# Passes over half of the queries, three banks for the maxima, and one exponential per head's bank

## What is computed

```
x = layer_norm(x, ln1)                      # the context, 6404 rows
lat = layer_norm(latents, ln2) * (1 + scale) + shift      # 1024 rows
q = lat @ Wq.T                              # 16 heads of 64
k, v = split(concat(x, lat) @ Wkv.T)        # 7428 keys
w = softmax((q / 64**0.25) @ (k / 64**0.25).T)
out = concat_heads(w @ v) @ Wo.T
```

## Time and profile before

| | us |
|---|---|
| median of 3 runs | 3836.62 (3833.6 to 3837.98) |
| the profiled execution | 3841.93 |
| its span, first to last instruction | 3840.2 |

### The profile page before, as it was taken

How to read it: one execution, slowest core, us unless ns; L and a number is a source line. 1 busy time by engine, 2 the same in 40 slices (tenths; PEclk the granted TensorE clock), 3 DMA queues, 4 the chain that set the end, 5 groups by cost and what they waited for, 6 DMA issues and landing times. The chain is left out here.

```text
span 3840.2 us, 51865 instructions
## 1 busy us (share of the span) xinstructions
PE 3356.3 (87%) x18323; PEld 1880.7 (49%) x18323; DVE 2607.8 (68%) x4176; ACT 1515.3 (39%) x1843; POOL 1641.2 (43%) x1061
## 2 busy tenths in 40 slices
PE   3896969668435699999999999999999999999977
PEld 2553636433232255555555555555555555554535
DVE  6887868765317877777777777778778778773221
ACT  4232313234220044444444444444444444444432
POOL 1222222201130055655555555556555555566650
PEclk9897969866666599999999999999999999999988
DMA  1000000000130000000000000000000000000000
GB/s 57 0 0 0 0 0 0 0 12 1 35 108 6 0 1 1 3 1 2 1 3 2 1 3 2 1 3 2 1 3 2 1 3 1 2 1 1 1 24 6
DMA packets 20389, 27.87 MB, mean 7 GB/s; under 512 B 5064, under 2 KB 12368, under 8 KB 20048
## 3 DMA queue, kind: packets, MB, share of 16 engines
q1 hardware_dynamic: 18832, 21.83, 1.8%
q0 software_dynamic: 1344, 3.15, 0.3%
HBM read 21.30 MB, written 3.67 MB: 7 GB/s over the span
## 5 line engine op out<-in xcount | busy, mean ns | idle before, releaser
L2140 POOL TENSOR_TENSOR pair_total_pool<-pair_total_pool,pair_probs 128x1024 f32<-128x1024 f32 (+2 forms) x456 | 1335.1, 2928 | 918.2 <-DVE pair_total L2104 880.0
L2027 ACT ACTIVATE pair_probs<-banks 128x1024 f32<-128x1024 f32 (+1 forms) x944 | 962.9, 1027 | 1137.0 <-PE banks L1921 1129.6
L2057 DVE TENSOR_REDUCE pair_peaks<-banks 128x1 f32<-128x512 f32 (+1 forms) x1680 | 1094.7, 673 | 238.6 <-PE banks L1902 198.2
L1945 PE MATMUL banks<-pair_probs,pair_values 128*64 128x512 f32 (+1 forms) x3776 | 863.1, 598 | 0.0
L1902 PE MATMUL banks<-pair_k_high,pair_q_high 64*128 64x512 f32 (+1 forms) x1920 | 706.4, 464 | 68.3 <-DVE pair_peaks L2050 51.1
L2104 DVE TENSOR_TENSOR pair_total<-pair_total,pair_probs 128x512 f32<-128x512 f32 x464 | 445.5, 960 | 208.2 <-POOL pair_total_pool L2140 155.6
L1902 PEld LDWEIGHTS banks<-pair_k_high,pair_q_high 64*128 64x128 f32 x1920 | 306.9, 195 | 443.4 <-issue 354.8
L1921 PE MATMUL banks<-pair_q_shift,pair_one_rows 64*128 64x512 f32 (+1 forms) x1888 | 512.8, 432 | 6.1 <-ACT pair_probs L2027 5.9
L1921 PE MATMUL banks<-pair_q_high,pair_k_high 64*128 64x512 f32 (+1 forms) x1888 | 494.1, 392 | 0.0
L1921 PE MATMUL banks<-pair_q_high,pair_k_low 64*128 64x512 f32 (+1 forms) x1888 | 493.2, 391 | 0.0
L1945 PEld LDWEIGHTS banks<-pair_probs,pair_values 128*64 128x64 f32 (+1 forms) x3776 | 249.4, 136 | 463.6 <-issue 400.6
(11 more groups left out here) (312 smaller groups left out, 3281.5 us busy)
## 6 DMA issues: line engine op xcount, KB each, us to landing
expert_w<-in_fc SPq DMA_DIRECT2D x32, 256.0 KB, 3.9
context_rows<-in_ctx SPq DMA_DIRECT2D x10, 320.0 KB, 6.2
dense_w<-in_We SPq DMA_DIRECT2D x2, 1024.0 KB
experts_in<-expert_zeros SPq DMA_DIRECT2D x1, 1024.0 KB, 3.9
expert_b<-in_fc_b SPq DMA_DIRECT2D x2, 512.0 KB
expert_rows<-experts_in SPq DMA_DIRECT2D x16, 64.0 KB, 2.0
experts_out<-expert_result POOLq DMA_DIRECT2D x4, 256.0 KB, 4.5
row_parameters<-in_rows SPq DMA_DIRECT2D x1, 896.0 KB, 7.9
```

Source lines behind the costliest of these rows:

```text
L1945: last = pe.matmul(out[heads[head], c, :], values[0:n, (g * BLOCKS + i // 4) % 2, i % 4, heads[head]], probs_of(i)[0:n, c, head, :], start ...
L2027: act.activation(probs_of(i)[0:n, c], slot(e)[0:n], ACT.Exp, scale=1.0 / 8.0).then_inc(S["expd"].sem, 1)
L2057: v.reduce_max(peaks[:, head, t, b:b + 1], fill_banks(f)[:, head, 0:width(b)], axis=AX).then_inc(S["peaked"].sem, 1)
L2140: pool.tensor_tensor(pooled[0:rows_, first:3], pooled[0:rows_, first:3], probs_of(i)[0:rows_].rearrange("p c h n -> p (c h) n")[:, first + ...
```

## The change

The loop over pairs becomes a loop over 16 **halves**: a half is one pair of heads by 512 of the 1024 queries (h = 2g and 2g + 1). Each half runs through all keys, with its own queries, maxima, shift, denominators and output, all 512 wide where they were 1024.

- **Steps.** 15 per half. A step is one block of keys: four tiles (three in the last, the third being the remnant) by 512 queries, so again four scores entries, each with one fill of the next half. 60 fills against 59 scores: one stands alone ahead of the scores of the last step. Before the first half 60 fills run alone instead of 120.
- **Banks.** `out` is 512 wide and needs one bank; banks 5, 6 and 7 hold the fills in turn, so a fill of one head waits for the maximum three before it, where it waited for the maximum of its own head in the fill before.
- **Exponentials.** One for each head's bank (512 columns), head 1 first (FIRST). The first waits for `half_made`, set by the last product of head 1, the second for `made`. The next user of the slot that is a scores entry waits at each head's first product for that head's exponential, not ahead of the entry; other users wait for both.
- **Places.** (0, 0), (1, 0), (1, 0), (2, 0) for tiles 0 to 3 of a block: head 1's fill first, head 0's at position 0, 1, 1 or 2 of its products.
- **Keys and values** of a pair serve both halves, so they are kept (a ring of 16 blocks each; values had two). Keys and values of pair g+1 are made in the odd half of pair g, values two blocks behind keys. Those of pair 0 are made in the stage in front, with the keys and under one signal.
- **Sums.** VectorE takes tile 0 of a block and one bank of tile 1 (at the end the remnant), POOL the rest in two operations; at a half's end POOL also adds VectorE's total and its own third part, in three operations in a row, and the denominators are two matmul sums instead of five.
- **Reciprocals** in four pieces (CHUNKS = 4), output in step 6 instead of step 10.

The core of the diff:

```diff
-STEPS1 = TILES // 2
-RING1 = BLOCKS + 3
-CHUNKS = 8
-FIFTH = (16, 18, 20, 22)
-PLACES = ((0, 0), (0, 3), (0, 3), (1, 4))
+HALVES = 2 * PAIRS
+TQ = TT // 2
+HALF = TQ * P
+LAST = BLOCKS - 1
+RING1 = BLOCKS + 1
+CHUNKS = 4
+PLACES = ((0, 0), (1, 0), (1, 0), (2, 0))
+FIRST = (1, 0)
...
-        order += [("fill", 0, b, t) for t in range(TT)]
+        order.append(("produce", 0, b + 1, 0, b) if b < LAST else ("produce", None, None, 0, b))
+        order += [("fill", 0, b, t) for t in range(TQ)]
...
+    for h in range(HALVES):
+        g, more = h // 2, h + 1 < HALVES
+        ahead = [("fill", h + 1, b, t) for b in range(BLOCKS) for t in range(TQ)] if more else []
+        for s in range(BLOCKS):
+            if s == LAST and more:
                 order.append(ahead.pop(0))
+            for i in tiles_of(s):
+                order.append(("scores", h, i, ahead.pop(0) if ahead else None))
+            made = [None] * 4
+            if h % 2 and g + 1 < PAIRS:
+                if s < LAST:
+                    made[0:2] = [g + 1, s + 1]
+                if s:
+                    made[2:4] = [g + 1, s - 1]
+            elif h % 2 == 0 and s == 0 and g:
+                made[2:4] = [g, LAST]
+            elif h % 2 == 0 and s == LAST and g + 1 < PAIRS:
+                made[0:2] = [g + 1, 0]
...
+            elif s == LAST:
+                adds = [("add", h, i) for i in tiles_of(s - 1)]
+                if more:
+                    order.append(("peak", h + 1))
+                if h + 2 < HALVES:
+                    order.append(("queries", h + 2))
+                order += adds[0:1] + produce + adds[1:2]
+                if more:
+                    order.append(("shift", h + 1))
+                order += adds[2:4]
...
-        values = k.sb("pair_values", [P, 2, 4, P], ctx=ctx)
+        values = k.sb("pair_values", [P, RING1, 4, P], ctx=ctx)
...
-        out = k.ps[:, 4:6, :]
+        out = k.ps[:, 4, :]
...
-        def fills_before(f):
-            return fill_number[f] - (1 if f[1] else 2)
+        def fill_bank(f, head):
+            return k.ps[:, 5 + (2 * fill_number[f] + FIRST.index(head)) % 3, :]
...
                 def fill(f, head):
...
+                    n = 2 * fill_number[f] + FIRST.index(head)
+                    if h:
+                        wait(pe, "peaked", max(n - 2, 2 * first_fills))
...
                     def product(head, m):
...
+                        if m == 0:
+                            wait_free(e, FIRST.index(head))
                         return pe.matmul(slot(e)[0:n, head, :], left, right, start=m == 0, stop=m == 3)
...
+                        elif turn == (FIRST[0], 3):
+                            product(*turn).then_inc(S["half_made"].sem, 1)
+                        elif turn == (FIRST[1], 3):
                             product(*turn).then_inc(S["made"].sem, 1)
...
+                    for head in FIRST:
+                        if head == FIRST[1]:
+                            wait_made(act, e)
+                        act.activation(probs_of(h, i)[0:n, head], slot(e)[0:n, head], ACT.Exp,
+                                       scale=1.0 / 8.0).then_inc(S["expd"].sem, 1)
```

## The result

The changed kernel takes 3732.1 us, median of four runs (3730.5 to 3736.0), where the kernel before took 3837.3 beside it: a ratio of 0.9728 (95% interval 0.9711 to 0.9744). 3728 was forecast. The profiled execution has a span of 3728.7 us against 3840.2, so 111.5 us less; the sum of the prediction had 108.5. In medians it is 105.2 us less, since the profiled execution before lay above the other runs and the one after was the fastest of its four.

The account below looks back on a forecast made before the run. PE was busy 87% but stopped by VectorE and ACT in turns; VectorE bound the front stage. Terms -51 - 15 - 52 + 7.5 + 7 - 5 = -108.5 gave 3728 us; 8-in-10 range 3665 to 3795.

Parts of the forecast that it names:

- Part 1: Front stage: four fewer maxima a block, keys' copy waits for values; blocks 11.1 to 8.1 us, together -51 us.
- the case that the prediction priced at -59: Front stage with PE at its full clock, where the values would cost 1.0 us a block.
- Parts 2 and 5: Last pair: values made a pair ahead, -15 us; shorter end, -5; its score phases +7.5, borders about +1.
- Part 3: Four scores of a step: 5.10 us, bounds 4.75 to 5.28; three-score phases 4.5; -52 us over seven pairs.
- the layout: Score phase timed slot by slot: VectorE's stops gone, third score waits for head 0's second exponential until 2.61, adds at 5.10.
- Part 4: Borders, twice as many: changes of form and 0 to 1 us waits before denominators, +7 us, bounds -5 and +25.
- the -46 of the forecast: Pairs 0 to 6: -52 us from score phases and about +6 for borders.
- A: Score phases: waits merely change place, phase stays 5.27, +36 us, 3764 us; chance 0.20.
- B: Score phases: no wait is left, -74 us, 3654 us; chance 0.12.
- C: Waits before each head's first product: even fulfilled, they stop weights loading ahead, 0.8 a phase, +168, 3896 us; chance 0.08.
- D: Borders: PE sits through POOL's whole chain, 6 us at each of 16, 3817 us; chance 0.05.

Follow-up runs that it names:

- experiment 6: Changed kernel with head 0's exponential first and, in the front stage, values as an entry of their own behind a block's second fill: 3674.1 us, 0.9568.
- experiment 2: Changed kernel with one exponential over both banks: first kernel, behind two waits in a row, 3759.4 us, 0.9795; second kernel, behind one wait, 3747.8 us, 0.9766.
- experiment 7: Kernel of experiment 6 with one of the four adds put ahead of the production in each step that has one: 3693.4 us, 0.9618.
- experiment 3: Changed kernel with two banks for maxima: 3820.2 us; two banks and the fills' old places, mirrored: 3779.0 us; three banks and those old places: 3734.9 us.
- experiment 1: Changed kernel with ACT making head 0's exponential first and PE asking for the banks in that order: 3704.8 us, 0.9656.
- experiment 5: Changed kernel with each head's wait for its exponential asked again ahead of its third product, eight more fulfilled waits a phase: 3728.7 us, 0.9716.

## Why the prediction was right

**Part 1, the front stage: -54.5 for -51.** The mechanism was as written, VectorE held by the keys' copy and that by the values, and experiment 6 shows it by taking it away. The blocks were 7.1 to 8.3, 7.9 in the mean, instead of 8.1; PE's clock, 0.67 in the mean, was not always the half one, toward the case that the prediction priced at -59.

**Parts 2 and 5, the last pair: -12.3 for -11.5.** The values gave the 15 (productions of this pair on PE fell from 16.2 us to 1.0), and from the last products on the end is 4.7 us shorter, for 5. The phases cost 9.4 (133.0 before, 142.4 after) for 7.5, and the rest is -1.8 for +1. One row was carried over wrongly: phases without fills were to stay 4.38 and are 4.47, 14 x 0.09 = 1.3 us. In the third score the two heads' first products, which start together before, now follow one another:

```profile
3521.01 0.92 PE L1925 MATMUL banks<-pair_q_shift,pair_one_rows 64*128 64x512 f32 x2
```

Head 1 is in its slot, 1.94 behind the phase's start, and head 0, whose exponential is the second, is 0.42 behind head 1. But with a wide one behind one wait (second kernel of experiment 2) these phases are still 4.44, so the split accounts for 0.03 of the 0.09. The 0.06 that the wide one has over 4.38 are about what its exponentials start later than in the kernel before.

**Part 3, the phase: 5.11 for 5.10.** Each step of the layout is there: no stop of the second score, head 1's fill in its slot at +2.40, head 0's product at +2.60 (2.61 was laid out), the fourth score free. The three-score phase is 4.42 for 4.5. VectorE no longer releases a regular fill; it does in the three-score phase, for the 0.40 us that were allowed:

```profile
3478.30 0.38 PE L1906 MATMUL banks<-pair_k_high,pair_q_high 64*128 64x260 f32 x1 [0.40 <-DVE pair_peaks L2069]
```

The sum of a pair's score phases after is 151.9 for 151.8. The one of before was put at 159.2 from the earlier trace rows and is 160.1 when all phases are added: one phase of each pair but the first, the one behind the output, was 5.97 and was taken for a regular one. So the phases gave -8.2 a pair, not -7.4.

**Part 4, borders: inside its bounds, but too low, and wrong in where it lies.** I allowed +7 for waits ahead of the denominators and for changes of form at the borders. The waits view of PE over all pairs (engine line waited for: us in total, times, longest us), of before and of after:

```profile
PE banks L1902 <- DVE pair_peaks L2057: 14.6, 65, 0.7
PE banks L1921 <- ACT pair_probs L2027: 5.9, 29, 0.2
```
```profile
PE banks L1964 <- POOL pair_total_pool L2134: 9.8, 8, 4.9
PE banks L1906 <- DVE pair_peaks L2069: 6.9, 16, 0.9
```

Less the 4.9 of the last one, which is the end of the stage, PE waits seven times for POOL, 0.7 us each, inside the 0 to 1 allowed, at every second border; and VectorE stops fills 16 times instead of 65. The denominators' fewer columns nearly paid for the changes of form and the wait: shift, queries, denominators and output take 7.5 us a pair before, and 7.3 after with 0.7 of waiting beside them, so +0.5 a pair for the +0.9 that was allowed. But adds and productions, which I had left alone, grew by 0.8 and 0.4 us a pair. More of their groups now stand between matmuls of another form: at a half's end the adds and the production are put among each other. The sixteen matmuls of a step's adds take 3.58 us where nothing stands between them, and at a half's end 1.01 + 1.01 + 1.87 = 3.89. No run takes this away alone, but experiment 7 puts one more such change in each step and pays 0.15 for it. One term was missing. Pair 0 had no border in it before, since nothing was finished ahead of it; now its second half has one, some 4 us, and pair 0 gives 2.1 us where the others give 6.5. From the -46 of the forecast for seven pairs: -6 that the phases gave beyond it, +9 of adds and productions, -2 of the allowance for borders, +4 of pair 0: -41, and -40.8 was measured.

**The sum was helped by luck.** Adds, productions and pair 0 were left out, 13 us that should have made the kernel slower than forecast. The phases gave 6 more than they were put at, the front stage 3.5, the borders 2, and stages that are the same in both kernels 3.8. That they nearly cancel was not foreseen. The layout of the phase and the mechanism of the front stage are what was right.

**The small rest:** 3.8 us are saved where nothing is changed, 2.8 of them ahead of the stage. They are 0.1% of the time and spread: ahead of the stage, where all these kernels are the same, the twelve profiled executions of before, after and the experiments reach it after 1160.5 to 1168.7 us.

**The rivals.** A, that the waits merely change place, would be 5.27: refuted by 5.11, and experiment 3 says which part keeps it from being so: with two banks the phase is 5.50 or 5.28. Without the split (experiment 2, one wait) it is 5.13 to 5.21. B, no wait left, is not reached even by experiment 1. C is refuted by experiment 5. D, at 6 us a border, met 0.7 at every second one.

**What I had wrong was in the expectations.** Experiment 2: a wide exponential was taken as free where VectorE no longer stops PE. It costs 16 us in this kernel, and the layout misses by what its exponentials start later than the rows of before have them; with the split, too, head 1 can run a slot ahead, which the wide one has to give up, and no run tells the two apart. Experiment 1: 27 us for 63, since the restart of the third score and the production behind an odd phase were not in the layout. Experiment 7: VectorE's idle time was read from regular steps, not from those that carry a reciprocal.

## What to carry to other kernels

When two engines hold the third by turns, remove both holds and then see what order the next wait is asked in: here the bank that is needed first was freed second, and turning that round gave a quarter of the change's gain again. Lay the phase out slot by slot from the rows of before; it gave 5.10 where 5.11 came, and a layout of *every kind* of phase (with a production behind it, with a reciprocal in it) would have told the misses too. An entry that bundles two results under one signal makes the reader of the first wait for the second.

## What the runs showed of the hardware

- From the start of a score's last products to the start of its exponential: 0.42 to 0.44 us for a 1024-wide one where one signal is given (kernel before), 0.42 for a 512-wide one that waits for the first of two signals, 0.45 to 0.46 for one that waits for the second (experiment 1), 0.47 to 0.51 for a 1024-wide one behind one wait for the second (experiment 2), 0.50 to 0.55 behind two waits in a row. A 1024-wide one takes 1.03 us; two 512-wide ones take 0.60 each and start 0.50 apart.
- Waits of PE that are already fulfilled cost nothing that can be seen, eight more in 5.11 us (experiment 5); a wait that ends just as the slot is due (0.04 late) makes the next slot 0.31 instead of 0.23 (experiment 1).
- The granted clock of the front stage, where VectorE has the most work, was 0.67 with blocks of 7.1 to 8.3 us and 0.96 with blocks of 5.33 (experiment 6).
- The same sixteen matmuls take 3.58 us in one group and 3.74 in two with another form of matmul between them (experiments 6 and 7).
- A bank more for what VectorE reads was worth 44 us with the old places of the fills and 88 with the new ones (experiment 3).
